# Reciprocal deviations in the combine and recurrence-input stages: ScalarE root, VectorE reciprocal and one Newton step in place of three Newton steps on GpSimd

## The reference, cut to what matters

```python
zn = layer_norm(z)                                  # over the 64 channels
a = sigmoid(zn @ w_ag + b_ag) * (zn @ w_ap + b_ap) * mask
b = sigmoid(zn @ w_bg + b_bg) * (zn @ w_bp + b_bp) * mask
p = einsum('bikc,bjkc->bijc', a, b)
out = (layer_norm(p) @ w_z + b_z) * sigmoid(zn @ w_g + b_g)
```

## Time and profile before

| | us |
|---|---|
| median of three runs (lowest, highest) | 2110.83 (2101.74, 2114.73) |
| profiled execution, first to last instruction (its span) | 2093.7 |
| what the median of the runs has beyond that span | 17.1 |
| PE / DVE / ACT / POOL busy | 1635.2 / 1490.1 / 1159.1 / 1127.2 |
| mean granted TensorE clock, share of full speed | 0.922 |

### The profile page before, as it was taken

The page is one execution under the profiler, slowest core; times in us unless marked ns, Lnnn a source line. Parts: engine busy times, 40 slices in busy tenths (PEclk is TensorE's granted clock), DMA queues, the critical chain, the costliest instruction groups (busy, mean ns, idle before and its releaser), DMA issues. The chain is left out here.

```text
span 2093.7 us, 38733 instructions
## 1 busy us (share of the span) xinstructions
PE 1635.2 (78%) x10716; PEld 1082.6 (52%) x10716; DVE 1490.1 (71%) x4816; ACT 1159.1 (55%) x2674; POOL 1127.2 (54%) x2090
## 2 busy tenths in 40 slices
PE   4777749986658779748877885998564899999997
PEld 2444438775544358624444445887564444444442
DVE  5888830557869968748778760256773899999996
ACT  5888835321117769627677772432114666666651
POOL 5878820466868810026656560066785566666652
PEclk9999979998879989959999997999985799999999
DMA  3778654787764306857888965488675566666652
GB/s 112 192 193 209 170 145 133 220 271 245 244 219 131 111 1 141 182 172 231 248 245 246 260 174 144 136 269 284 220 241 169 158 186 182 184 184 183 184 150 83
DMA packets 456027, 390.18 MB, mean 186 GB/s; under 512 B 221232, under 2 KB 369328, under 8 KB 455856
## 3 DMA queue, kind: packets, MB, share of 16 engines
q1 hardware_dynamic: 410800, 321.07, 54.5%
q10 hardware_dynamic: 45056, 67.13, 9.9%
HBM read 203.55 MB, written 150.99 MB: 169 GB/s over the span
## 5 line engine op out<-in xcount | busy, mean ns | idle before, releaser
L524 PE MATMUL cp_pv<-cp_weight,cp_zt 64*128 64x320 f32 x2048 | 368.8, 468 | 106.0 <-ACT cp_zt L462 88.8
L348 DVE SCALAR_TENSOR_TENSOR a_res<-cp_pv,cp_mask,cp_sig 128x64 f32<-128x64 f32 x1024 | 263.7, 322 | 124.1 <-ACT cp_sig L471 119.6
L1506 DVE TENSOR_TENSOR ex_xe<-ex_spread,ex_xd 128x512 f32<-128x512 f32 x512 | 317.5, 682 | 20.5 <-PE ex_spread L1757 17.5
L471 ACT ACTIVATE cp_sig<-cp_pv 128x384 f32<-128x384 f32 x512 | 249.8, 492 | 125.9 <-PE cp_pv L524 125.5
L524 PEld LDWEIGHTS cp_pv<-cp_weight,cp_zt 64*128 64x128 f32 x2048 | 184.5, 189 | 224.4 <-issue 195.3
L695 PE MATMUL cc_sum<-a_res,cc_room 128*128 128x256 f32 x1024 | 240.2, 388 | 24.0 <-DMA cc_room<-b_scratch 23.9
L1773 PE MATMUL ex_po<-ex_xe,ex_expert 128*64 128x512 f32 x1024 | 249.5, 609 | 0.0
L695 PEld LDWEIGHTS cc_sum<-a_res,cc_room 128*128 128x128 f32 x1024 | 198.7, 199 | 52.4 <-DMA cc_room<-b_scratch 33.4
L451 ACT ACTIVATE cp_xn<-cp_x,cp_lift,cp_rstd 128x64 f32<-128x64 f32 x512 | 196.2, 438 | 53.4 <-POOL cp_lift L399 53.4
L1628 ACT ACTIVATE ex_xn<-ex_x,ex_lift,ex_rstd 128x64 f32<-128x64 f32 x512 | 182.0, 429 | 20.9 <-POOL ex_lift L1550 20.9
L426 POOL TENSOR_TENSOR cp_b_stage<-cp_b_stage,cp_mask 128x256 f32<-128x256 f32 x256 | 151.4, 612 | 64.9 <-DVE cp_b_stage L350 64.8
(11 more groups left out here) (196 smaller groups left out, 3361.5 us busy)
## 6 DMA issues: line engine op xcount, KB each, us to landing
gate_scratch<-cp_sig SPq DMA_DIRECT2D x128, 256.0 KB, 2.6
b_scratch<-cp_b_stage SPq DMA_DIRECT2D x128, 256.0 KB, 3.9
cc_room<-b_scratch SPq DMA_DIRECT2D x128, 256.0 KB, 2.7
ex_xd<-ex_xt SPq DMA_DIRECT2D x256, 128.0 KB, 2.6
cp_x<-in_x SPq DMA_DIRECT2D x64, 256.0 KB, 3.2
cc_room<-gate_scratch ACTq DMA_DIRECT2D x64, 256.0 KB, 4.0
cc_p<-in_x SPq DMA_DIRECT2D x64, 256.0 KB, 3.9
after_conv<-cc_p ACTq DMA_DIRECT2D x64, 256.0 KB, 3.4
```

The lines of the kernel that those rows point to most:

```text
L348: dve.scalar_tensor_tensor(a_res[:, h, :, row], bank[:, h, 3 * C:4 * C], mask_sb[:, h, row:row + 1], sig[u.mod(2)][:, 0, h, i, :], ALU.mul ...
L471: act.activation(sig[u.mod(2)][:, :, :, i, :].rearrange("p k h c -> p h k c"), pv[slot(u, i)][:, :, 0:3 * C].rearrange("p h (k c) -> p h k ...
L524: pe.matmul(pv[slot(u, i)][:, h, 0:COLS], zt[u.mod(2)][half, i * P:(i + 1) * P], weight[half, :], start=True, stop=True).then_inc(v_made, 1)
L1506: dve.tensor_tensor(xe[u.mod(2)][:, :, h, i * P:(i + 1) * P], pb[k][:].rearrange("p (e t) -> p e t", e=EP), xd[u.mod(8)][:, h, i * P:(i + ...
```

## The change

In both functions `first_guess` becomes `halve` (only `half_var` is made), ScalarE makes the square root of twice that (`deviate`), and VectorE makes its reciprocal and one Newton step of three operations (`invert`). GpSimd makes no roots any more here. In combine, `invert(q)` stands in DVE's list behind `scale(4q-2)`, and `deviate(q)` in ACT's list behind `take_flipped(4q-3)`. In the recurrence's inputs, GpSimd normalises all four units of a four (VectorE none), `half_var` gets a second buffer, `invert(f)` stands behind `measure(4f+4)`, and `deviate(f)` ahead of `take(4f-4)`. The other stages stay as they are.

```diff
-def newton(pool, numbers, guess, half_var, root, rstd, done, base):
...
+def newton(dve, guess, half_var, root, rstd, done, base):
+    dve.tensor_tensor(root, guess, guess, ALU.mult).then_inc(done, 1)
+    dve.wait_ge(done, base + 1)
+    dve.tensor_tensor(root, root, half_var, ALU.mult).then_inc(done, 1)
+    dve.wait_ge(done, base + 2)
+    dve.scalar_tensor_tensor(rstd, root, 1.5, guess, ALU.subtract, ALU.mult, reverse0=True).then_inc(done, 1)
...
 conv_combine
-    ROOTS = 12
+    ROOTS = 3
...
-                def first_guess(quad):
+                def halve(quad):
                     dve.wait_ge(counted, quad * 4 + 4)
                     if quad:
                         dve.wait_ge(refined, quad * ROOTS)
                     dve.tensor_scalar(half_var[:], stats[:, :, :, 2].rearrange("p n i -> p (n i)"), 0.5 / C, 0.5e-5,
-                                      ALU.mult, ALU.add).then_inc(guessed, 1)
-                    dve.wait_ge(guessed, quad * 3 + 1)
-                    dve.tensor_scalar(shifted[:], half_var[:].bitcast(I32), 1, None, ALU.logical_shift_right
-                                      ).then_inc(guessed, 1)
-                    dve.wait_ge(guessed, quad * 3 + 2)
-                    dve.tensor_scalar(guess[:], shifted[:], -1, MAGIC, ALU.mult, ALU.add).then_inc(guessed, 1)
+                                      ALU.mult, ALU.add).then_inc(halved, 1)
+                def invert(quad):
+                    dve.wait_ge(rooted, quad + 1)
+                    dve.reciprocal(guess[:], deviation[:]).then_inc(guessed, 1)
+                    dve.wait_ge(guessed, quad + 1)
+                    newton(dve, guess[:], half_var[:], root[:], rstd[quad % 2][:].rearrange("p n i -> p (n i)"),
+                           refined, quad * ROOTS)
...
                 for n in range(LEAD):
                     measure(n)
+                    if n == 4:
+                        invert(0)
                 for n in range(LAST):
                     scale(n)
+                    if n % 4 == 2 and n + 4 < LAST:
+                        invert(n // 4 + 1)
                     if n + LEAD < LAST:
                         measure(n + LEAD)
...
-                refine(0)
                 for n in range(LAST):
-                    if n % 4 == 2 and n + 4 < LAST:
-                        refine(n // 4 + 1)
                     for g in gated_in(n):
                         add(g)
...
+                def deviate(quad):
+                    act.wait_ge(halved, quad + 1)
+                    act.activation(deviation[:], half_var[:], ACT.Sqrt, scale=2.0).then_inc(rooted, 1)
...
                 fetch_gate(0)
                 fetch_gate(1)
+                deviate(0)
                 for k in range(CHUNKS, CHUNKS + AHEAD):
                     take_sums(k)
...
                     take_flipped(n)
+                    if n % 4 == 1:
+                        deviate(n // 4 + 1)
...
 scan_input
-    ON_DVE = 1
+        half_var = [m.sb(f"half_var{q}", [P, 4 * T]) for q in range(2)]
...
+                def invert(four):
+                    dve.wait_ge(rooted, four + 1)
+                    if four >= 2:
+                        dve.wait_ge(xn_made, (four - 1) * 4)
+                    dve.reciprocal(guess[:], deviation[:]).then_inc(guessed, 1)
...
                     if s == 3:
                         fold()
-                    for u in range(4 * (s // 4) - 4, 4 * (s // 4)):
-                        if s % 4 == 2 and 0 <= u < G and on_dve(u):
-                            normalise(dve, u).then_inc(xn_dve, 1)
+                        invert(0)
+                    elif s % 4 == 0 and 4 < s <= G:
+                        invert(s // 4 - 1)
                     count(s - LATE)
...
+                    pool.wait_ge(refined, (four + 1) * ROOTS)
+                    for u in range(four * 4, four * 4 + 4):
+                        if u >= 4:
+                            pool.wait_ge(xt_made, u - 3)
+                        pool.tensor_tensor(xn[u % 4][:], xs[u % NX][:].rearrange("p h i c -> p i h c"),
...
+                def deviate(four):
+                    act.wait_ge(halved, four + 1)
+                    if four:
+                        act.wait_ge(guessed, four)
+                    act.activation(deviation[:], half_var[four % 2][:], ACT.Sqrt, scale=2.0).then_inc(rooted, 1)
+                deviate(0)
+                deviate(1)
                 take(0)
                 for u in range(1, G):
+                    if u % 4 == 0 and u + 4 < G:
+                        deviate(u // 4 + 1)
                     take(u)
                     take_wx(u - 1)
```

More of the change, by code:

```diff
@@ L743, in measure @@
                     if n % 4 == 3:
[L744 to L746 removed]
+                        halve(n // 4)
+                def halve(quad):
                     dve.wait_ge(counted, quad * 4 + 4)
@@ L787, in _ @@
             def _(pool):
[L788 to L793, removed]
                 def add(n):
@@ L854, in _ @@
                     take_flipped(n)
+                    if n % 4 == 1 and n // 4 + 1 < LAST // 4:
+                        deviate(n // 4 + 1)
                     if n + 5 >= STEPS + LATE_GATES:
@@ L985, in measure, with halve @@
                     if u % 4 == 3:
[L986 to L988 removed]
+                        halve(u // 4)
+                def halve(four):
                     dve.wait_ge(counted, four * 4 + 4)
[L991 to L999 removed]
+                    if four >= 2:
+                        dve.wait_ge(refined, (four - 1) * ROOTS)
+                    dve.tensor_scalar(half_var[four % 2][:].rearrange("p (u t) -> p u t", t=T), stats[four % 2][:, :, :, 2],
+                                      0.5 / C, 0.5e-5, ALU.mult, ALU.add).then_inc(halved, 1)
+                def invert(four):
+                    dve.wait_ge(rooted, four + 1)
+                    if four >= 2:
+                        dve.wait_ge(xn_made, (four - 1) * 4)
+                    dve.reciprocal(guess[:], deviation[:]).then_inc(guessed, 1)
+                    dve.wait_ge(guessed, four + 1)
+                    newton(dve, guess[:], half_var[four % 2][:], root[:], rstd[four % 2][:].rearrange("p u t -> p (u t)"),
+                           refined, four * ROOTS)
                 def count(u):
@@ L1040, in _ @@
                 for four in range(FOURS):
-                    pool.wait_ge(guessed, four * 3 + 3)
-                    if ON_DVE and four >= 2:
-                        pool.wait_ge(xn_dve, (four - 1) * ON_DVE)
-                    newton(pool, numbers, guess[:].bitcast(F32), half_var[:], root[:],
-                           rstd[four % 2][:].rearrange("p u t -> p (u t)"), refined, four * ROOTS)
-                    for u in range(four * 4, four * 4 + 4 - ON_DVE):
-                        normalise(pool, u).then_inc(xn_pool, 1)
+                    pool.wait_ge(refined, (four + 1) * ROOTS)
[3 more added lines that the diff above has]
+                        pool.tensor_tensor(xn[u % 4][:], xs[u % NX][:].rearrange("p h i c -> p i h c"),
+                                           over(rstd[four % 2][:, u % 4, :].rearrange("p (i h) -> p i h", h=H), C),
+                                           ALU.mult).then_inc(xn_made, 1)
                 pool.wait_ge(end, 6)
```

53 lines of the change are left out of this document (15 added, 38 removed).

## The result

| | before | after |
|---|---|---|
| median (lowest, highest; four runs each) | 2106.51 (2101.74, 2114.73) | 2050.08 (2043.37, 2055.34) |
| ratio, 95% interval | | 0.9734 [0.9699, 0.977] |
| profiled span | 2093.7 | 2046.4 |

The change made the kernel 2.7% faster. The prediction said 2072.8 us with a range of 2044 to 2098: the direction and the range were right, and the value was 22.7 us too high. By medians 56.4 us went, by the two profiled spans 47.3, where I had summed 38. The difference of 9.1 us can be put to no stage: the trace of before is of an execution some 11 us quicker than its median, the trace of after of one some 2 us quicker (estimates, from the 1.8 us that the later runs have around their spans).

The account below looks back on a forecast made before the run. Bounds: VectorE in the recurrence's inputs, a DVE-POOL chain in combine's second half, waits for gate DMAs in the first. Terms -20 - 6 - 13 + 1 = -38 us took 2110.8 to 2072.8 us, range 2044 to 2098.

Parts of the forecast that it names:

- the first rival: Both combine halves and si: POOL's add doesn't hold up `invert`, which costs 0.85 us, giving 2048 us; chance 0.16.
- the lock: Of a POOL and a DVE operation that both read two tensors from SBUF, the second waits for the first.
- -20 said: Combine's second half, both stages: 44.8 us removed, 25.2 added by `invert`, a gain of 20 us (bounds 15 to 33).
- All three removals: Second half: waits for `cc_rstd` 25.8 us, scales slowed by an add 14.7, shift and guess 4.3.
- the wait of the first product: Second half: `invert`'s products wait for POOL's add, so `invert` holds DVE 1.8 us rather than 0.9.
- -13 said: Recurrence's inputs: a four falls from 7.93 to 7.0 us, over 14 fours a gain of 13 us (bounds 6, 16).
- -6 said: Combine's first half: 0.4 us a quad over 16 quads, a gain of 6 us (bounds: loss of 7, gain of 15).
- +1 said: ScalarE: four more table loads (cc0, sc, cc1, ex) cost 1 us in all (0 to 5.1).
- The reciprocal: 0.25 said: `invert` on DVE: the reciprocal alone takes 0.25 us, with bounds of 0.18 and 0.68.
- Products that each wait for a POOL operation: Combine and si: each `invert` product waits for a whole POOL operation, `invert` 4.7 and 4.5 us, total 2182; chance 0.04.
- DMAs that take over the second half: Second-half quads end at 12.3 us near the 275 GB/s rate, first half gains nothing, total 2090 us; chance 0.14.
- A root that doesn't stay cheap: ScalarE: each of 48 roots needs two table loads, 2.57 us, total 2118 us; chance 0.06.

Follow-up runs that it names:

- e1: Kernel after with the combine stages put back as before, only the recurrence's inputs changed: 2085.01 us, ratio to before 0.9921.
- f2: Kernel after without ScalarE root and reciprocal; VectorE makes the bits' guess and all three Newton steps: 2126.45 us, ratio to before 1.0099.

## Why the prediction was right, and where it was not

**The whole.** 2050.08 us is inside the stated range, but under the forecast's own 2057 to 2088. It lies closest to the first rival's 2048, and that rival is not what happened: the lock was met, and the first halves did not come free. Part of the distance is the step from span to median (13.4 of 22.7 us, below), part two terms that were sized too low. That the range held is owed to its lower edge, which that rival had set, and is in part luck; the direction and the stages that gain are not.

**Second half: mechanism right, size low (-20 said, -28.4 measured).** All three removals and the wait of the first product came where I put them. Each quad gained 1.87 us and not 1.43, and at 11.16 it lies just under the 11.3 to 11.9 that I gave. `invert` was 1.59, not 1.8: I let the first product run its 0.22 after the add's end, where it ends 0.05 behind it, so from the add's end to the next operation it was 530.29 - 529.87 = 0.42 and not 0.66. The shift and the guess freed 0.42, not 0.31. The saved wait was 1.97 in this quad where the mean of 25.8 over 14 is 1.84. And it is worth 28.4 / 1.87 = 15 quads, not the 14 I counted.

**Recurrence's inputs: -13 said, -18.5 measured.** `invert` was 0.95 in the sum and 0.94 in the trace. The mis-sized term is `half_var` with shift and guess: I let 0.31 + 0.17 us go. The rows had the answer: from `half_var` to the next operation it was 679.35 - 678.49 = 0.86, and now it is 641.37 - 641.28 = 0.09. So 0.77 went, since POOL is idle there now and nothing dependent follows. That makes 6.68 and not 7.0, under my 6.9 to 7.2.

**First half: -6 said, -3.8 measured, and the reason was wrong.** The size says little, as after and the combine-only run differ there by 4.1 and 7.9 us with the same code. I hid `invert` under DVE's wait for the gate, and I priced it without that cover at 0.9 us, without the lock, which the first product meets there too. The run with three steps on VectorE shows that the wait is hardly a cover: its `invert` is 3.39 - 1.59 = 1.80 us longer, which is 28.8 over 16 quads, and its first halves (202.8 and 228.4 us) are 29.0 longer than those of after (191.5 and 210.7). The step on GpSimd (187.3 and 207.6) differs from after by 4.2 and 3.1, no more than this scatter. The third buffer fits a reason: the gate's DMA is late because the add before it is late, and the add waits for DVE's gate product, so a delay on DVE goes once round the loop and comes back as a later DMA. That `invert` took there what POOL's Newton steps gave back is my reading; no run separates the two.

**Table loads: +1 said, up to 2.2 shown.** The experts' stage takes 503.6 to 504.7 us in all eight kernels whose combine stages make roots, and 501.5 to 502.6 in the three that don't (before, e1, f2): 2.2 us by the means. Its load (L1660) stands on ACT right behind a copy, at 1574.27, in a stretch where ACT rests some 0.65 us in every 4. The load is 1.28 of the 2.2; where the rest comes from is not shown. In sc, kernels with and without a load ahead of it overlap (116.9 to 119.7, and 117.4 and 117.6), so the +1.9 of the table is not the load's: it ran at 721.04 to 722.32 us, and the operation behind it waited until 725.18. At the first root, the load began at 365.87 and ended 2.2 us before the root (369.37), which waited for `halve`, so it was free, as the earlier trace rows had suggested. The Trainium skill (ScalarE: Activation LUTs, section "What ACT_TABLE_LOAD costs") adds a drain of some 1380 ns to each load's 1283; the 1283 agrees with every load here, but between two loads 1.51 us apart (536.08 and 537.59) there is room for the load, the small sigmoid and no drain.

**The reciprocal: 0.25 said, 0.34 measured.** That is within the bounds of 0.18 and 0.68. The estimate from the Trainium skill (VectorE: DVE Perf Modes, section "First, the fixed hardware budget"), by which its repeat count of 8 would add 0.27 us, to 0.52, is not borne out: it exceeds a product of the same size, at 0.19, by 0.15. (The 0.27 is also the whole of 32 x 8 cycles, so as an addition to the 0.25, which already holds the 32 elements, it counts part of them twice.)

**Rivals.** Products that each wait for a POOL operation: only the first one waits. DMAs that take over the second half: they run at 283 GB/s and no wait there ends on a DMA. A lock that isn't met: it is, and taking it away was worth another 0.68 us a quad. A root that doesn't stay cheap: four loads in all; the run with 96 of them was slower than before, at 2136.12 us, more than the 2118 I had for it.

**From span to median.** I added 17.1 us for what lies around the span. Every run since lists its own span, which is 1.7 to 1.9 us below its time (after: 2046.4 and 2048.23). With the same 1.8, the profiled execution of before took some 2095.5 us, an estimate, and was quicker than all three timed ones (2101.74 at the least): the 17.1 was mostly that. After has 3.7 there. So 13.4 of the 22.7 us of error come from this step, and 47.3 - 38 = 9.3 from the stages: 8.4 from the second half and 5.5 from si, less what the first half, sc and the experts kept back.

## What to carry to other kernels

When a piece of work leaves an engine's list, ask first how long the engine that takes it is already busy in that stage: here fewer steps gained, and the move to the full engine gave part of it back, which a run with the same steps on the idle engine showed. An idle wait inside a closed loop of buffers (fetch, use, store, fetch again) was hardly a cover for new work in that loop here, and one more buffer (24 us in the two first halves) was worth more there than the cheaper arithmetic. A table load that is cheap where ScalarE waits is dear where it stands behind a copy that ends after the data is there. Small operations that depend on each other and share a reading path with another engine are priced from the start of the first to the start of the next unrelated one, never from their own lengths, and they are put where the other engine is idle or beside an operation that reads one tensor.

## What was not expected of the hardware

- A shift of integers on DVE that reads only one tensor took 1.21 us beside POOL's add and 0.18 elsewhere (the earlier trace rows and the run with three steps on VectorE), while a reciprocal of one tensor ran in 0.33 beside the same add. So the number of tensors read doesn't alone decide who waits. The Trainium skill (SBUF — State Buffer, section "Who interferes with whom") has operations of a tensor with a scalar among those that can take the path shared with GpSimd though they read one tensor; the shift agrees with it.
- GpSimd's operations of 128x32 on two tensors cost little more than VectorE's: 0.24 to 0.26 us against 0.19, when nothing is beside them.
- The first half of combine moved 318 to 321 GB/s with a third buffer, where 275 to 279 had looked like a limit.
